# The setup of a one-core kernel's long convolution, cut into eight passes and put between the stages of its first two trips

## The chip, the cores and the metric

One core of a Trainium2 chip runs the whole program. The core has five engines, each with a queue of its own that is worked off in order: TensorE (PE: matmuls, and PEld: its weight loads), VectorE (DVE), ScalarE (ACT), GpSimd (POOL) and SyncE (SP), which here issues nearly all DMAs. They meet at semaphores. The time is the device time in microseconds (us) of one execution: 1694.19 us, the median of 3 runs (1694.01 to 1695.35).

## The reference

Eight sequences of 512 tokens with 256 channels go through two layers, each an attention part and a feed-forward part, with residuals:

```python
x = x + L0_xattn(layernorm(x), ctx, ...)  # 8 heads, 64 context rows, softmax
x = x + L0_ffn(layernorm(x), ...)         # 16 experts of 64, the best 4 by a sigmoid gate
x = x + L1_xattn(layernorm(x), ctx, ...)  # below
x = x + L1_ffn(layernorm(x), ...)         # 8 experts of 1024, each takes the 512 best of 4096 rows
```

The third part attends to the context with the best 32 of 64 scores in each of 4 heads, makes a scale and a shift from it (FiLM), runs a long convolution over the sequence, then FiLM again, a gelu layer and a layernorm. The kernel of the convolution depends on weights alone, not on `x`:

```python
dtA = dt[:, None] * A                      # 256 channels x 64 complex states
dC = C * (jnp.exp(dtA) - 1.0) / A
powers = jnp.exp(dtA[:, :, None] * jnp.arange(L))
K = 2.0 * jnp.einsum('dn,dnl->dl', dC, powers).real
y = irfft(rfft(x, n=2 * L) * rfft(K, n=2 * L))[:, :L] + x * D_skip
```

## The kernel before, in words

The program has three blocks with a barrier between them.

The first, `setup_block` (L113), makes what depends on weights alone. SyncE loads the parameters of the convolution and then all weights (L169 to L189). VectorE computes steps and coefficients on 128x256 tiles (L282 to L318). Then the powers are made in four passes of 64 channels, each as a product of a wide factor (32 steps of 16 tokens, 128x2048) and a narrow one (16 tokens, 128x1024): VectorE makes the phases (`phases`, L329: the products L332 and L334, the rounding L325 and L326), GpSimd the exponents (L232), ScalarE takes sines (L409 to L411) and exponentials (L413, L414), VectorE multiplies them (`powers`, L338), and TensorE sums over the states with 64 small matmuls (L437). Between passes 2 and 3 weights are centred (so that the layernorms' means drop out of the products): TensorE L444 and L456, ScalarE L418 to L426. At the end the taps are transposed twice (L462, L468), transformed (L474) and folded into `kf` (L387 and the adds behind it).

The second, `layers_block`, runs the batches as a pipeline of trips. A batch passes three phases, ATTEND (L0 attention and its gates), MID (L0 feed-forward, L1 attention scores and the best-32 picking) and LAST (FiLM, convolution, gelu layer, scores for the experts), and is in one of them in each trip. One hand-written list, `ORDER`, gives the order in which every engine's queue gets the stages of the three batches; `take_stages` (L496) walks it. The first trip has an ATTEND batch alone, the second an ATTEND and a MID batch, six trips have all three, then come a trip with MID and LAST and one with LAST alone. Stages by name: `soften` (row maximum, subtraction, sum), `attend` (scores, Exp, transposes of the probabilities), `attend_out` and `attend_sum`, `route` and `gates`, `spread` (gates to DRAM and back, spread over partitions as `gT`), `mlp` and `relu`, `pick` (16 in a batch: MAX8 and MATCH_REPLACE, L991 and L995), `picked`, `film`, `transform`, `product`, `back`, `gelu`, `ffn_out`. In PSUM, banks 0 to 3 belong to ATTEND and `mlp`, 4 and 5 to MID, 6 and 7 to LAST.

The first products of a trip's `film` stage are two transposes of `am` (L1408), one for each half; where a trip is said to begin here, it is with one of them. Matmuls of these stages carry one line, L1283, transposes L1289; they are told apart by their tiles (`ps<-m,xT`: attention scores; `ps<-hT,vo`: attention output; `ps<-x,keys` and `ps<-hT,values`: the feed-forward; `ps<-w,big`: `ffn_out`; `ps<-wfilm,v1T`: stage `text` part 2).

The third, `experts_block`, chooses the rows of each expert and runs the eight experts. The change does not touch it.

## Time and profile before

| what | us |
|---|---|
| median of 3 runs | 1694.19 |
| the profiled execution: its own time | 1691.25 |
| its span, first to last instruction | 1689.1 |
| setup block | 0 to 178.0 |
| first trip (ATTEND) | 178.0 to 230.6 |
| second trip (ATTEND, MID), until the second `am` transposes of the third | 230.6 to 343.63 |
| one of the six full trips | 140.2 |
| MID and LAST trip | 110.2 |
| LAST alone | 98.2 |
| experts | 1390.7 to the end |

Busy shares over the span: PE 79%, PEld 48%, DVE 55%, ACT 28%, POOL 19%. A row of a timeline gives start, duration, engine, line, output<-inputs, shapes and count, and in brackets how long the engine had been idle before and what it waited for. Float32 matmuls show two records each. The granted clock of TensorE is 1.00 at 2.4 GHz and 0.50 at 1.2 GHz.

### The profile page before, as it was taken

Reading aid. Unit: us, or ns where it says so; the run is one execution under the profiler, and the core shown is the slowest. Engines: PE = TensorE matmul, PEld = TensorE weight load, DVE = VectorE, ACT = ScalarE, POOL = GpSimd, SP = SyncE. Lnnn points to the kernel's source line nnn. Section 1 sums busy time; section 2 is a strip of 40 time slices with the busy share of each in tenths; the row PEclk is TensorE's granted clock in tenths of the full one; section 3 lists DMA queues with packets and bytes.
Section 4 is the critical chain, followed back from the end, with each engine's and each line's share of the span. In section 5 each row is a group of like instructions: output and inputs, shape, how many; then the busy total and the mean of one; then the engine's idle time right before and its main releaser. Section 6 shows DMA issues by size and latency. Waiting matters only on the chain. (4 is left out here: it accounts for less than half of the span.)

```text
span 1689.1 us, 17636 instructions
## 1 busy us (share of the span) xinstructions
PE 1330.4 (79%) x5358; PEld 810.5 (48%) x5358; DVE 929.4 (55%) x3400; ACT 480.8 (28%) x823; POOL 327.1 (19%) x592
## 2 busy tenths in 40 slices
PE   0265669699889979979988997997995551999997
PEld 0245434345545555455554554545543240667674
DVE  6955414777576567666757656766666428211111
ACT  0433201214322521621532342162142223332221
POOL 3210100203101120320320112022022120433322
PEclk9995779799979969979997996997996675899999
DMA  8000020020020020002003002001200005243511
GB/s 261 2 0 1 2 63 15 14 50 15 14 76 16 12 78 15 1 26 64 16 13 77 16 13 76 14 1 23 54 1 26 1 32 183 67 116 82 144 17 21
DMA packets 44856, 72.55 MB, mean 43 GB/s; under 512 B 8085, under 2 KB 26648, under 8 KB 44634
## 3 DMA queue, kind: packets, MB, share of 16 engines
q1 hardware_dynamic: 38618, 62.90, 12.7%
q0 software_dynamic: 6144, 8.52, 2.9%
q8 instruction: 43, 0.70, 0.2%
q14 instruction: 51, 0.42, 0.1%
HBM read 58.31 MB, written 13.11 MB: 42 GB/s over the span
## 5 line engine op out<-in xcount | busy, mean ns | idle before, releaser
L770 POOL TENSOR_SCALAR ve<-mv 128x2 f32<-128x2 f32 x80 | 18.1, 227 | 854.1 <-DVE mv L868 853.9
L1283 PE MATMUL ps<-x,keys 128*128 128x512 f32 x256 | 137.1, 662 | 11.1 <-DVE hT L954 11.1
L1283 PE MATMUL ps<-zT_second,w 128*128 128x512 f32 x256 | 119.1, 602 | 3.7 <-ACT big L1249 2.4
L1366 PE MATMUL ps<-hT,values 128*128 128x512 f32 x256 | 119.1, 593 | 0.0
L1809 PE MATMUL experts_ps<-experts_yT,experts_fc 128*128 128x512 f32 x256 | 113.5, 602 | 1.3 <-ACT experts_yT L1732 1.3
L1283 PE MATMUL ps<-w,big 128*128 128x256 f32 x512 | 113.6, 381 | 0.8 <-ACT big L1249 0.8
L1821 PE MATMUL experts_ps<-experts_fc,experts_hT 128*128 128x256 f32 x512 | 112.1, 380 | 0.8 <-ACT experts_hT L1744 0.8
L1283 PEld LDWEIGHTS ps<-w,big 128*128 128x128 f32 x512 | 96.6, 190 | 22.7 <-issue 8.5
L1821 PEld LDWEIGHTS experts_ps<-experts_fc,experts_hT 128*128 128x128 f32 x512 | 96.6, 190 | 14.7 <-ACT experts_hT L1744 1.6
L437 PE MATMUL pk<-setup_WA,setup_U 128*32 128x16 f32 x512 | 27.9, 214 | 93.5 <-DVE setup_WA L346 93.5
L1707 DVE SCALAR_TENSOR_TENSOR experts_o<-experts_ps,experts_wh,experts_b2w 128x256 f32<-128x256 f32 x32 | 15.5, 484 | 140.2 <-PE experts_ps L1821 140.2
L1283 PE MATMUL ps<-vf,amT 65*128 65x512 f32 x128 | 80.9, 744 | 14.4 <-ACT amT L1139 13.6
L1283 PEld LDWEIGHTS ps<-x,keys 128*128 128x128 f32 x256 | 51.8, 210 | 78.3 <-issue 57.0
L1744 ACT ACTIVATE experts_hT<-experts_ps,experts_b 128x512 f32<-128x512 f32 x64 | 44.0, 687 | 157.3 <-PE experts_ps L1809 157.3
L954 DVE SCALAR_TENSOR_TENSOR hT<-ps,gT 128x512 f32<-128x512 f32 x64 | 42.6, 687 | 78.8 <-PE ps L1283 62.9
L1587 POOL DMA_INDIRECT out_x<-experts_o,experts_idx x32 | 51.4, 1606 | 157.1 <-DVE experts_o L1707 155.2
L1366 PEld LDWEIGHTS ps<-hT,values 128*128 128x128 f32 x256 | 48.8, 191 | 62.1 <-issue 58.2
L1809 PEld LDWEIGHTS experts_ps<-experts_yT,experts_fc 128*128 128x128 f32 x256 | 48.8, 193 | 60.4 <-issue 60.2
L995 DVE MATCH_REPLACE8 work<-rest,work 128x64 f32<-128x64 f32 x384 | 76.0, 209 | 0.2 <-issue 0.2
L900 DVE SCALAR_TENSOR_TENSOR x<-ps,b_oT,xT 128x512 f32<-128x512 f32 x16 | 12.0, 751 | 111.8 <-PE ps L1283 111.8
L437 PEld LDWEIGHTS pk<-setup_WA,setup_U 128*32 128x32 f32 x512 | 27.6, 157 | 93.7 <-issue 93.7
L1283 PEld LDWEIGHTS ps<-zT_second,w 128*128 128x128 f32 x256 | 46.0, 193 | 48.3 <-issue 42.0
(382 smaller groups left out, 2590.7 us busy)
## 6 DMA issues: line engine op xcount, KB each, us to landing
gT<-expert_gates SPq DMA_DIRECT2D x16, 1024.0 KB, 9.7
experts_fc<-in_fc1T SPq DMA_DIRECT2D x8, 1024.0 KB, 5.4
experts_fc<-in_fc2T SPq DMA_DIRECT2D x8, 1024.0 KB, 9.6
expert_table<-tb SPq DMA_DIRECT2D x8, 528.0 KB, 12.2
x<-in_x SPq DMA_DIRECT2D x8, 512.0 KB, 3.5
xT<-in_xT SPq DMA_DIRECT2D x8, 512.0 KB, 3.6
out_x<-x SPq DMA_DIRECT2D x8, 512.0 KB, 11.5
w<-in_W SPq DMA_DIRECT2D x2, 1024.0 KB, 13.5
```

What stands on the lines that cost most here:

```text
L437: last = nc.tensor.matmul(pk[q * LI:(q + 1) * LI, half, at:at + LJ], Us[q % 2][:, d, :], WAs[q % 2][:, d, :], start=True, stop=True)
L770: nc.gpsimd.tensor_scalar(o, i, c, None, ALU.add).then_inc(*tick(*event))
L900: nc.vector.scalar_tensor_tensor(xp[:, k, :], bank("OT", k), S["b_oT"][:, k:k + 1], xT[:, k, :], ALU.add, ALU.add).then_inc(*tick("emptied ...
L954: nc.vector.scalar_tensor_tensor(hT[:, c % RING, :], bank("H", c), 0.0, gT[:, c, :], ALU.max, ALU.mult).then_inc(*tick("emptied", "H", c))
L995: nc.vector.match_replace(work[:, t, h, :], best[:, h, :], src[:, h, :], OUT_OF_RANGE).then_inc(*tick("tmr", t, n, h))
L1283: last = nc.tensor.matmul(o, l, r_, start=start, stop=stop)
L1366: last = nc.tensor.matmul(bank("O2", k), S["values"][:, c, k * P:(k + 1) * P], hT[:, c % RING, :], start=(c == 0), stop=(c == HC - 1))
L1587: g.indirect_dma_start(out_rows, bass.IndirectOffsetOnAxis(ap=idx[:, e, c:c + 1], axis=0), o[e % 2][:, c, :], None, compute_op=ALU.add).th ...
L1707: nc.vector.scalar_tensor_tensor(o[s][:, c, :], o_bank(CC * e + c), wh[s][:, c:c + 1], b2w[s][:, c, :], ALU.mult, ALU.add).then_inc(out_ma ...
L1744: nc.scalar.activation(hT[e % 2][:, m, :], g_bank(m), ACT.Gelu_apprx_tanh, bias=b1[:, e, m:m + 1]).then_inc(hidden_made, 1)
L1809: last = nc.tensor.matmul(g_bank(m), fc1[e % 3][:, k, m * P:(m + 1) * P], yT[e % 2][:, k, :], start=(k == 0), stop=(k == DC - 1))
L1821: last = nc.tensor.matmul(o_bank(at), hT[e % 2][:, m, c * P:(c + 1) * P], fc2[e % 3][:, m, :], start=(m == 0), stop=(m == HC - 1))
```

## The change

`setup_block` goes. Its buffers are laid over tiles that the first two trips do not use yet (`big`, `xf`, `yv`, `x3`, `tb`, `zT_second`, `work`), and it uses PSUM banks 4 to 7 until the stages of MID and LAST need them. Its work becomes stages of a fourth phase, `KERN`: `steps`, `means`, `masks`, `phases` p and `powers` p (p from 0 to 7, 32 channels each, so tiles of 128x1024 and 128x512), `centre` 0 to 5, `bias`, `fold_film`, `film_row`, and `kernel` 0 to 5 (transposes, transform and folding). Loads get a semaphore for each group in place of one for all, with waits `if first(b)` where the first batch uses them. There are five stage lists now: `FIRST` (ATTEND and KERN up to `powers` 3), `SECOND` (ATTEND, MID and the rest of KERN), `ORDER`, changed in places, for the six full trips, `DRAIN` and `FINAL`. In `FIRST` the stages stand in this order: steps 0, keys 0, steps 1, means, phases 0, centre 0, powers 0, phases 1, masks, keys 1, keys 2, phases 2, centre 1, norm, attend 0, centre 2, soften 0, powers 1, attend 1, attend 2, soften 1, centre 3, soften 2, soften 3, attend 3, bias, attend 4, soften 4, phases 3, attend_out, attend_sum, centre 4, route, powers 2, gates 0, fold_film, gates 1, centre 5, gates 2, phases 4, gates 3, spread, film_row, powers 3. `SECOND` begins text 0, mlp 0, phases 5, text 1, mlp 1, powers 4, relu 0 to 2.

TensorE's queue from the program's start before, all of the setup up to the transform's transposes:

```order
L437 MATMUL pk<-setup_WA,setup_U 32x16 x128
L444 MATMUL pc<-b_ffn,w 128x1 x16
L456 MATMUL pc<-keys,setup_cen 128x512 x8
L456 MATMUL pc<-w,setup_cen 128x512 x8
L456 MATMUL pc<-sel,setup_cen 128x16 x4
L456 MATMUL pc<-gate_w,setup_cen 128x8 x4
L437 MATMUL pk<-setup_WA,setup_U 32x16 x128
L462 MATMUL pt<-ident,setup_kq 64x128 x16
```

And now, in the first trip, from the first batch's first score product; `xf,big` are the 32 matmuls of one pass (powers 1), `keys,work` and `gate_w,work` are centring, `b_ffn,w` is the bias:

```order
L1336 MATMUL ps<-mrow,ones_bf 128x512
L1336 MATMUL ps<-m,xT 128x512 x2
L1381 MATMUL ps<-keys,work 128x512 x4
L1353 MATMUL ps<-xf,big 32x16 x32
L1336 MATMUL ps<-mrow,ones_bf 128x512
L1336 MATMUL ps<-m,xT 128x512 x2
L1342 MATMUL ps<-ident,e_buf 128x128 x4
L1336 MATMUL ps<-mrow,ones_bf 128x512
L1336 MATMUL ps<-m,xT 128x512 x2
L1342 MATMUL ps<-ident,e_buf 128x128 x4
L1381 MATMUL ps<-gate_w,work 128x8 x4
```

The matmuls of the passes, 128 in a row before, now stand by 32 between the score products, with the centring beside them.

VectorE's queue at the start of the second trip now: phases 5, powers 4 (rows L697 to L785 with `xf`, `yv`) and the first six `relu` rows (`hT<-ps,gT`), phases 6 behind them:

```order
L763 SCALAR_TENSOR_TENSOR xf<-tb,yv 128x512
L762 TENSOR_SCALAR tb<-yv,offB 128x512
L763 SCALAR_TENSOR_TENSOR yv<-tb,yv 128x512
L697 TENSOR_TENSOR xf<-xf,zT_second 128x512
L697 TENSOR_TENSOR yv<-yv,zT_second 128x512
L700 TENSOR_TENSOR xf<-xf,yv 128x512
L784 TENSOR_TENSOR big<-big 128x1024
L785 TENSOR_TENSOR xf<-xf,x 128x512
L942 SCALAR_TENSOR_TENSOR hT<-ps,gT 128x512 x6
L771 TENSOR_TENSOR big<-zT_second,it_i 128x1024
L762 TENSOR_SCALAR tb<-big,offA 128x1024
L763 SCALAR_TENSOR_TENSOR big<-tb,big 128x1024
```

Before, the `relu` rows followed the gates' last row with only two small copies between.

In a full trip, TensorE before, at the end of the gelu layer's first product:

```order
L1283 MATMUL ps<-zT_second,w 128x512 x2
L1289 MATMUL ps<-ident,e_buf 128x128 x4
L1283 MATMUL ps<-zT_second,w 128x512 x4
L1283 MATMUL ps<-wfilm,v1T 64x512 x4
L1283 MATMUL ps<-w,big 128x256 x16
L1283 MATMUL ps<-hT,vo 128x512 x8
```

and now:

```order
L1336 MATMUL ps<-zT_second,w 128x512 x2
L1336 MATMUL ps<-wfilm,v1T 64x512 x4
L1342 MATMUL ps<-ident,e_buf 128x128 x4
L1336 MATMUL ps<-zT_second,w 128x512 x4
L1336 MATMUL ps<-w,big 128x256 x16
L1336 MATMUL ps<-hT,vo 128x512 x8
```

The four matmuls of `text` part 2 moved ahead of the last transposes of the probabilities. On VectorE in the same trips `norm_out` 0 now stands ahead of the three last `pick` stages that follow `attend_sum`.

```diff
-def setup_block(nc, ctx, S, A, tally):
...
+ATTEND, MID, LAST, KERN = range(4)
...
+PASSES, PC = 8, 32
...
+FIRST = [
+    (KERN, "steps", 0), (ATTEND, "keys", 0), (KERN, "steps", 1), (KERN, "means"), (KERN, "phases", 0), (KERN, "centre", 0),
...
+SECOND = [
...
+    (MID, "relu", 1), (MID, "relu", 2), (MID, "mlp", 2), (MID, "mlp", 3), (MID, "relu", 3), (MID, "mlp", 4), (MID, "mlp", 5),
...
+            sp.dma_start(ctx0[:], ctx_h[0]).then_inc(*tick("ctx0_loaded"))
+            load("wk", kv_in)
+            load("wv", kv_in)
+            for rows_ in (slice(0, NS), slice(NS, P)):
+                for dst, src in ((are, A["A_reT"]), (aim, A["A_imT"]), (cre, A["C_reT"]), (cim, A["C_imT"])):
+                    sp.dma_start(dst[rows_, :], src).then_inc(par_in, 16)
+            sp.dma_start(ldt, A["log_dt"].partition_broadcast(P)).then_inc(par_in, 16)
...
-            take_stages(stages, 0, None, None)
-            take_stages(stages, 1, 0, None)
+            take_stages(stages, FIRST, 0, None, None, 0)
+            take_stages(stages, SECOND, 1, 0, None, 0)
             for b in range(B - 2):
-                take_stages(stages, b + 2, b + 1, b)
-            take_stages(stages, None, B - 1, B - 2)
-            take_stages(stages, None, None, B - 1)
+                take_stages(stages, ORDER, b + 2, b + 1, b, None)
+            take_stages(stages, DRAIN, None, B - 1, B - 2, None)
...
+            def phases(_, p):
+                if p == 0:
+                    g.wait_ge(*at(0, "k_coef"))
+                else:
+                    g.wait_ge(*at(0, "k_ex", p - 1))
+                if p >= 2:
+                    g.wait_ge(*at(0, "k_pow", p - 2))
+                some = decay[:, p * PC:(p + 1) * PC].unsqueeze(2)
+                g.tensor_tensor(UEs[p % 2], some.to_broadcast([P, PC, LI]), it_i[:].unsqueeze(1).to_broadcast([P, PC, LI]), ALU.mult)
+                g.tensor_tensor(WEs[p % 2], some.to_broadcast([P, PC, LJ]), it_j[:].unsqueeze(1).to_broadcast([P, PC, LJ]),
+                                ALU.mult).then_inc(*tick("k_ex", p))
...
+            def phases(_, p):
+                k = p % 2
+                wide = spare[:, 0:PC * LI].rearrange("p (d i) -> p d i", i=LI)
+                narrow = spare[:, 0:PC * LJ].rearrange("p (d j) -> p d j", j=LJ)
+                if p >= 2:
+                    v.wait_ge(*at(0, "k_taps", p - 2))
+                step(nc.vector.tensor_tensor(Us[k], over(spin, p, LI), it_i[:].unsqueeze(1).to_broadcast([P, PC, LI]), ALU.mult))
+                step(whole_less(Us[k], Us[k], offA[:], wide))
+                step(nc.vector.tensor_tensor(WBs[k], over(spin, p, LJ), it_j[:].unsqueeze(1).to_broadcast([P, PC, LJ]), ALU.mult))
+                step(whole_less(WAs[k], WBs[k], offA[:], narrow))
+                whole_less(WBs[k], WBs[k], offB[:], narrow).then_inc(*tick("k_phase", p))
+
+            def powers(_, p):
+                k = p % 2
+                v.wait_ge(*at(0, "k_sin", p))
+                mul(WAs[k], WAs[k], over(alpha, p, LJ))
+                mul(WBs[k], WBs[k], over(beta, p, LJ))
+                add(WAs[k], WAs[k], WBs[k])
+                v.wait_ge(*at(0, "k_exp", p))
+                nc.vector.tensor_tensor(Us[k], Us[k], UEs[k], ALU.mult)
+                nc.vector.tensor_tensor(WAs[k], WAs[k], WEs[k], ALU.mult).then_inc(*tick("k_pow", p))
+
+            def means(_):
...
+            def bias(_):
+                v.wait_ge(bias_filled, 1)
+                v.wait_ge(w1_in, 80)
+                nc.vector.tensor_tensor(S["b1"][:], S["b1"][:], pc[:, 0, 0:HC], ALU.add).then_inc(bias_made, 1)
...
+            def phases(_, p):
+                k = p % 2
+                if p == 0:
+                    a.wait_ge(*at(0, "k_coef"))
+                a.wait_ge(*at(0, "k_phase", p))
+                nc.scalar.activation(Us[k], Us[k], ACT.Sin, scale=-TWO_PI, bias=sinA[:])
+                nc.scalar.activation(WAs[k], WAs[k], ACT.Sin, scale=-TWO_PI, bias=sinA[:])
+                nc.scalar.activation(WBs[k], WBs[k], ACT.Sin, scale=-TWO_PI, bias=sinB[:]).then_inc(*tick("k_sin", p))
+
+            def powers(_, p):
+                k = p % 2
+                a.wait_ge(*at(0, "k_ex", p))
+                nc.scalar.activation(UEs[k], UEs[k], ACT.Exp)
+                nc.scalar.activation(WEs[k], WEs[k], ACT.Exp).then_inc(*tick("k_exp", p))
+
...
+            def powers(_, p):
+                lanes = slice((p // 2) * LI, (p // 2 + 1) * LI)
+                pe.wait_ge(*at(0, "k_pow", p))
+                for d in range(PC):
+                    last = nc.tensor.matmul(pk[lanes, p % 2, d * LJ:(d + 1) * LJ], Us[p % 2][:, d, :], WAs[p % 2][:, d, :], start=True, stop=True)
+                last.then_inc(*tick("k_taps", p))
+
...
-            setup_block(nc, ctx, S, A, None)
```

## Rows read from the trace of the kernel before

**Rows 1.** Windows by stage: us, busy time (instructions) per engine, granted clock, DMA share, GB/s
```profile
core 0: us, PE busy (x) PEld busy (x) DVE busy (x) ACT busy (x) POOL busy (x), PEclk, DMA share, GB/s
0.00:178.00 178.00, 65.11 (x640) 51.92 (x640) 117.03 (x118) 50.56 (x47) 36.70 (x37) 0.87 0.20 63
178.00:230.60 52.60, 38.06 (x145) 24.86 (x146) 16.75 (x55) 10.24 (x19) 7.30 (x10) 0.76 0.04 12
230.60:343.63 113.03, 84.43 (x272) 43.66 (x272) 56.11 (x283) 18.44 (x38) 12.54 (x26) 0.82 0.18 42
613.29:753.50 140.21, 124.77 (x446) 73.17 (x445) 91.17 (x377) 46.08 (x81) 25.54 (x58) 0.90 0.12 32
```
**Rows 2.** Timeline, a 64-channel pass beside GpSimd and alone: start us, us, engine, line
```profile
32.53 3.63 POOL L232 TENSOR_TENSOR setup_UE<-setup_decay,setup_it_i 128x2048 f32<-128x2048 f32 x1 [25.81 <-DVEq L318]
32.54 5.77 DVE L332 TENSOR_TENSOR setup_U<-setup_turn,setup_it_i 128x2048 f32<-128x2048 f32 x1
38.35 2.83 DVE L325 TENSOR_SCALAR setup_US<-setup_U,setup_offA 128x2048 f32<-128x2048 f32 x1
41.21 5.60 DVE L326 SCALAR_TENSOR_TENSOR setup_U<-setup_US,setup_U 128x2048 f32<-128x2048 f32 x1
50.50 1.22 DVE L326 SCALAR_TENSOR_TENSOR setup_WA<-setup_WS,setup_W 128x1024 f32<-128x1024 f32 x1
53.81 2.29 DVE L332 TENSOR_TENSOR setup_U<-setup_turn,setup_it_i 128x2048 f32<-128x2048 f32 x1
56.14 1.29 DVE L325 TENSOR_SCALAR setup_US<-setup_U,setup_offA 128x2048 f32<-128x2048 f32 x1
```
**Rows 3.** Timeline, VectorE on 512 columns
```profile
171.58 0.69 DVE L257 TENSOR_TENSOR setup_U<-pt,setup_US 128x512 f32<-128x512 f32 x1
```
**Rows 4.** Timeline, ScalarE in the passes
```profile
57.91 1.28 ACT L413 ACT_TABLE_LOAD   x1
59.20 1.91 ACT L413 ACTIVATE setup_UE<-setup_UE 128x2048 f32<-128x2048 f32 x1
67.05 1.13 ACT L410 ACTIVATE setup_WA<-setup_WA,setup_sinA 128x1024 f32<-128x1024 f32 x1
```
**Rows 5.** Timeline, TensorE in the setup
```profile
72.37 6.98 PE L437 MATMUL pk<-setup_WA,setup_U 128*32 128x16 f32 x128 [72.37 <-DVE setup_WA L346]
87.68 6.99 PE L444 MATMUL pc<-b_ffn,w 128*128 128x1 f32 x32
```
**Rows 6.** Timeline of the first two trips
```profile
191.18 1.98 PE L1283 MATMUL ps<-m,xT 128*128 128x512 f32 x4
209.52 8.94 PE L1283 MATMUL ps<-hT,vo 128*128 128x512 f32 x16 [0.68 <-ACT hT L1139]
230.83 0.57 ACT L1139 COPY lists<-ps 16x512 f32<-16x512 f32 x1 [5.10 <-PE ps L1289]
245.80 1.29 DVE L954 SCALAR_TENSOR_TENSOR hT<-ps,gT 128x512 f32<-128x512 f32 x2 [15.88 <-DMA gT<-expert_gates]
343.63 0.38 PE L1408 MATMUL ps<-ident,am 128*64 128x128 f32 x2
```
**Rows 7.** Windows, one of the first trip, three of a steady trip
```profile
208.00:212.00 4.00, 3.32 (x7) 1.61 (x7) 0.00 (x0) 0.59 (x1) 0.00 (x0) 0.50 0.02 4
613.29:633.00 19.71, 17.34 (x47) 9.57 (x46) 9.42 (x30) 3.44 (x8) 0.00 (x0) 0.67 0.63 164
633.00:730.00 97.00, 92.80 (x317) 50.83 (x316) 62.07 (x250) 34.91 (x57) 15.62 (x30) 1.00 0.03 8
730.00:753.50 23.50, 14.64 (x85) 12.77 (x85) 19.68 (x99) 7.72 (x17) 9.91 (x28) 0.69 0.06 21
```
**Rows 8.** Waits of TensorE in one steady trip (613.29 to 753.5)
```profile
PE ps L1289 <- DVE x L1118: 4.8, 1, 4.8
PE ps L1289 <- DVE sct L1126: 3.4, 1, 3.4
```
**Rows 9.** Timeline, the last transposes of the probabilities in that trip
```profile
705.76 0.66 PE L1289 MATMUL ps<-ident,e_buf 128*128 128x128 f32 x4 [0.76 <-POOL e_buf L794]
```

790 lines of the change are left out of this document (425 added, 365 removed).

## The prediction
> **What bounds the kernel now.** I read the busy time by stage first, because a share over the whole span mixes stages with different limits. In the setup VectorE is busy 117.03 of 178.00 us and TensorE 65.11; in the first trip they stand at 16.75 and 38.06 of 52.60, in the second (until the second `am` transposes of the third trip) at 56.11 and 84.43 of 113.03; in a full trip at 91.17 and 124.77 of 140.21 [rows 1]. So the setup is VectorE's, the trips are TensorE's, and up to 343.63 us [rows 6] neither is full: VectorE works 117.03 + 16.75 + 56.11 = 189.9 us there, TensorE 187.6. The two kinds of work have different limits and don't need each other until `kf` is used by the first LAST batch. The experts, from 1390.7 on, keep their work and their time.
>
> Next I read the timeline of the passes, for what one instruction costs beside other engines and alone; then that of the first two trips, for the places where VectorE stands still; then the granted clock in the trips; last the waits of TensorE in a steady trip.
>
> **The change part by part.** The reference point is the second `am` transposes of the third trip, 343.63 us before. I sum up VectorE's time to it, since everything in the new front passes through its queue.
>
> *Start.* VectorE's first product on the parameters can begin at about 12 us. Its loads now stand behind three others, but before it worked through the masks first, so the start is where it was. Term: 12.
>
> *VectorE's work.* 189.9 us move over [rows 1]. In it are slow instructions: in the first pass VectorE ran beside GpSimd's exponents, and the wide product took 5.77 us where the next pass, alone, took 2.29; the subtraction's two rows took 2.83 against 1.29 and 5.60 against 2.29 [rows 2]. That is 3.48 + 1.54 + 3.31 = 8.3 us, which I take out and price anew below: 181.6. Eight passes in place of four double the count at half the size. 128x1024 takes 1.22 us where 128x2048 takes 2.29 [rows 2], so two halves cost 0.15 more than one whole, and 128x512 takes 0.69 [rows 3], so two cost 0.16 more. With some eleven such instructions in an old pass that is 4 x 11 x 0.16 = 7. The 44 more instructions have a gap of their own to the one that they depend on, and the centring's copies and the steps are cut finer: I take 13 for these, an estimate, with 5 and 20 as its ends. Term: 181.6 + 20 = 202.
>
> *Contention with GpSimd.* One old pass lost 8.3 us while GpSimd made the exponents of two old passes, which are four new ones: 2.1 each. GpSimd now makes the exponents of pass p + 1 just as VectorE's phases or powers run, so I count all eight: 16. Below, it could be 4 (only the first two); above, 22. The rows show the wide product longer by 3.48 us beside a GpSimd product of 3.63 [rows 2], so it lost nearly all of the other's duration. The Trainium skill, "SBUF — State Buffer", section "Who interferes with whom", calls the port pair that the two share an exclusive lock; the trace agrees. By that rule each new pass costs VectorE the full duration of GpSimd's two products, an estimate of 2.8 us, 22 in all, and the sum would be 6 us higher.
>
> *VectorE's waits.* These replace the old ones (15.88 us for the gates' DMA before the first `relu` [rows 6], the serial ends of the setup). That DMA wait is hidden in the new order: phases 5 and powers 4, some 12 us of VectorE work, stand in front of `relu` 0. What is late instead, in turn:
> - `powers` p waits for ScalarE's exponentials, which stand behind the sines of pass p + 1. A 128x1024 sine takes 1.13, a table load 1.28, a 128x2048 exponential 1.91 [rows 4], half of it about 1.04. Wide and two narrow sines 2.4, load 1.3, two exponentials 1.6 make 5.3; VectorE covers its three narrow products, 2.1, and in some passes norm or softmax work too. I take 2.5 x 8 = 20 (ends 5 and 35).
> - The first batch's softmax waits for scores that stand behind taps 1 and a centring product: 32 matmuls of a half pass are 3.5, half of 6.98 [rows 5]; the centring's four 512-column products and the scores' own cost about 4 and 1.98 [rows 6]. 9.
> - The bias is 6.99 us of TensorE [rows 5] put between scores 3 and 4; soften 4 waits for most of it. 6.
> - Attention output, 8.94 at the low clock [rows 6], and gates: 3 + 2, the rest lies beside phases 3 and 4.
> - phases 5 waits for taps 3: 3.5 [rows 5].
> - `relu` in the second trip: two key and two value products of 1.98 against 1.29 of VectorE per step [rows 6], 2.7 x 4 = 10, less where a pass stands between them.
> - Second batch: pick 0 2.8, scores behind taps 6 and 7 3.5 each, the first kernel transform 2.9. 12.7.
> Together 66 us, of which the last five items, some 46, are TensorE's own speed.
>
> ScalarE's table switches multiply: Sin and Exp alternate in every pass, with Exp of the softmax between. The row shows the load for 1.28 us and the exponential 0.01 us behind it [rows 4]. The Trainium skill, "ScalarE: Activation LUTs", section "What ACT_TABLE_LOAD costs", gives about 1.28 us for the load and 1.38 more for a drain at each switch; on the load the trace agrees, a drain of that size does not follow it in the row. If it were paid ahead of each load, some seven switches on VectorE's path would make the sum 10 us higher.
>
> *The clock.* In the first two trips TensorE was granted 0.76 and 0.82 on average [rows 1], which means that it ran at half rate for 48% and 36% of the time: 208 to 212 shows 0.50 with TensorE busy 3.32 of 4 us [rows 7]. In the new front TensorE's work is thinner, 188 us spread over some 300. If two fifths of the 46 us above are at the low level where I priced them at the high one, the cost is 18; several prices above already hold slow rows (8.94). I take 10 (ends 0 and 20).
>
> Sum: 12 + 202 + 16 + 66 + 10 = 306 us against 343.63, that is -38.
>
> *Steady trips.* TensorE waits 0.76 us for GpSimd's probabilities ahead of their last transposes [rows 9]; `text`'s four products now stand there and fill it. `norm_out` 0 earlier on VectorE lets GpSimd make the second half's `rstd` about 0.7 us earlier, which the 4.8 us wait for `x` (L1118) gets [rows 8]. So about 1.5 us less in a trip by the instructions. But a trip ends and starts at a granted clock of 0.69 and 0.67 and runs at 1.00 between [rows 7]; where that stretch begins and ends isn't set by these two edits. I take half, -0.8 x 6 = -5 (ends -10 and 0). The last two trips, with lists of their own: an estimate of -1, for waits of VectorE like those of [rows 8] that such a trip no longer has.
>
> **Total.** -38 - 5 - 1 = -44. The profiled execution took 1691.25 us (span 1689.1 and 2.15 around it) and becomes 1647. The median of the runs is 2.94 above that execution, so the prediction is 1650.
>
> **The rivals.**
>
> *Better covered.* The waits are 46 instead of 66, the rest stands (12 + 202 + 16 + 46 + 10 = 286): VectorE has norms, gate work and masks to do while ScalarE makes the exponentials, which my walk along the queues may place wrongly. For it: the old order shows idle TensorE and idle VectorE in the same stretches, and the softmax stages are short. Against: the queues are in order, and most `powers` stand right behind VectorE's short stages. Time 1630.
>
> *VectorE alone.* Waits of 40 and no half-rate term: 12 + 202 + 16 + 40 = 270, time 1650 - 36 = 1614. For it: 202 + 16 = 218 us of work is already four fifths of that. Against: the bias, taps and first attention are TensorE's and serial for the first batch.
>
> *The clock keeps the front low, and the trips give nothing.* TensorE in short pieces between waits is granted half rate for most of the front: the 46 us of its items take about 12 more than I priced, front 318; and the steady trips stay at 140.2. Then -26 - 1 = -27 and the time is 1668. For it: 0.76 in the first trip, where TensorE was busy 72% of the time. A front whose passes run one after another because each reuses the buffers of the pass two before would end here too.
>
> *Slower.* The moved products open a second half-rate stretch in every full trip. From 633 to 730 TensorE is at 1.00 with 92.80 of 97 us busy [rows 7]; were 7.5 us of that work at half rate, a trip would take 7.5 longer. It decides from the point at which the six trips lose what the front gains, 38 + 1 over 6 = 6.5 us a trip. With 7.5 us a trip the sum is -38 - 1 + 45 = +6, time 1700. For it: such stretches exist at each trip's ends. Against: the edit takes idle time out of this stretch, it adds none.
>
> **How the numbers follow.** Forecast 1650: 0.47. Better covered, 1630: 0.20. VectorE alone, 1614: 0.12. Low clock in the front, 1668: 0.17. Slower, 1700: 0.04. From the unknown costs of the likeliest case, ends of the powers' waits (-15, +15), contention (-12, +6), gaps (-8, +7), clock (-10, +10) and trips (-5, +5), which won't all fall on one side, its own range is 1636 to 1662. To hold eight of ten it must take in the second case and most of the fourth, and half of the third: 1618 to 1670. A measurement of this kernel tells about 0.2% (3.4 us) from no change; every case but the last is far beyond it: faster 0.95, within 0.01, slower 0.04.
>
> **What would show it.** The second `am` transposes of the third trip stand at about 306 us; at 270 or 286 a better case holds, at 318 or more the clock's. VectorE waits for ScalarE's exponentials about 2.5 us in a `powers` stage, and its wide products of phases take over 1.22 us (up to 3) in most passes; if they take 1.22, the contention term is wrong. Right ahead of `relu` 0 there is no long wait for the gates' DMA; if there is, the spread's DMA is late and my hiding of it fails. The bias keeps VectorE waiting before soften 4. A full trip takes 139.4, within 1 us; one of 147 is the slower case. The experts block takes 298 us as before; if it moves, the whole account is incomplete.

## The result, and the profile after

The changed kernel takes 1686.93 us (median of 5, 1685.06 to 1687.38) against 1695.35 (5 runs, 1694.01 to 1697.18) of the kernel before on the same chip: 0.9947 of it, interval 0.9932 to 0.9961, or 8.4 us less. I had forecast 1650, in a range of 1618 to 1670. The direction was right; the size was five times too large.

The stages of the profiled execution (span 1685.6), columns as in [rows 1]: the front (everything up to the second `am` transposes of the third trip) in two pieces, one of the usual full trips, the one unusual trip, the MID and LAST trip, the last trip, the experts.

```profile
core 0: us, PE busy (x) PEld busy (x) DVE busy (x) ACT busy (x) POOL busy (x), PEclk, DMA share, GB/s
0.00:178.00 178.00, 107.56 (x595) 69.73 (x596) 107.56 (x180) 59.14 (x83) 43.16 (x53) 0.82 0.26 78
178.00:312.00 134.00, 90.81 (x461) 56.97 (x460) 89.32 (x326) 29.87 (x47) 15.46 (x28) 0.76 0.10 25
601.37:744.94 143.57, 127.67 (x446) 75.02 (x445) 91.17 (x375) 43.94 (x78) 25.85 (x58) 0.88 0.12 31
889.25:1027.70 138.45, 122.72 (x445) 72.15 (x444) 90.94 (x375) 43.59 (x78) 25.70 (x58) 0.92 0.12 33
1171.23:1284.76 113.53, 95.47 (x297) 53.86 (x296) 74.95 (x322) 28.95 (x55) 18.96 (x48) 0.89 0.10 30
1284.76:1383.86 99.10, 58.34 (x178) 36.75 (x178) 35.45 (x91) 19.00 (x35) 12.82 (x33) 0.72 0.03 11
1383.86:1685.60 301.74, 244.37 (x1166) 162.82 (x1166) 81.76 (x282) 77.28 (x149) 86.15 (x91) 0.90 0.34 89
```

The balance against the profiled execution before:

| stretch | before | after | difference | forecast |
|---|---|---|---|---|
| front | 343.6 | 312.0 | -31.6 | -38 |
| six full trips | 838.7 | 859.2 | +20.6 | -5 |
| MID and LAST trip | 110.2 | 113.5 | +3.3 | -1, with the next |
| LAST trip | 98.4 | 99.1 | +0.7 | |
| experts | 298.2 | 301.7 | +3.5 | 0 |
| span | 1689.1 | 1685.6 | -3.5 | -44 |

(Rounded rows; the last two trips end where the experts' first load is issued. The profiled execution before was 4.1 us under the median of its five runs and the one after 0.5 above, so the balance shows 3.9 us of the 8.4.) The front did nearly what I had said. Two thirds of its gain was given back in the trips that I had expected to gain by moves in their own list: 138.2 and then five times 140.0 to 140.2 us before, now 145.9, 143.5, 143.6, 144.3, 138.5, 143.5. Work didn't grow: VectorE is busy 91.17 us in either [rows 1], while TensorE is busy 127.67 instead of 124.77 with the same number of instructions and a mean granted clock of 0.88 instead of 0.90.

The trip of 138.5 must be held against its like. The kernel before has one too, its first full trip, at the same clock of 0.92:

```profile
343.63:481.85 138.22, 122.96 (x445) 71.89 (x445) 91.48 (x376) 46.04 (x80) 25.55 (x58) 0.92 0.08 21
```

So at the same clock the new list is 0.2 us longer than the old one, not shorter. The lengths go with the time that the clock stands at 0.50 in a trip: 22.9 and 23.0 us in the trips of 138.2 and 138.5, 27.4 in those of 140.1, 34.3 in those of 143.5.

Where the clock went shows in windows of four us. First two stretches of the trip that starts at 601.37, then the same two of the trip that starts at 889.25:

```profile
609.37:613.37 4.00, 4.00 (x20) 2.66 (x19) 2.29 (x5) 0.26 (x1) 0.00 (x0) 1.00 0.06 20
613.37:617.37 4.00, 2.79 (x10) 1.87 (x10) 3.90 (x8) 1.67 (x6) 0.00 (x0) 0.78 0.00 0
617.37:621.37 4.00, 4.00 (x9) 1.80 (x8) 4.00 (x11) 0.00 (x0) 0.00 (x0) 0.80 0.00 0
681.37:685.37 4.00, 0.91 (x5) 0.87 (x5) 3.88 (x26) 3.46 (x5) 2.54 (x6) 0.81 0.00 0
685.37:689.37 4.00, 4.00 (x9) 1.44 (x8) 3.86 (x31) 3.82 (x8) 1.04 (x1) 0.76 0.00 0
897.25:901.25 4.00, 2.79 (x17) 1.93 (x16) 4.00 (x8) 1.08 (x5) 0.00 (x0) 1.00 0.09 35
901.25:905.25 4.00, 4.00 (x12) 2.19 (x12) 3.90 (x9) 0.60 (x1) 0.00 (x0) 1.00 0.00 0
965.25:969.25 4.00, 0.92 (x5) 0.49 (x5) 3.50 (x23) 3.09 (x5) 2.83 (x8) 1.00 0.00 0
969.25:973.25 4.00, 4.00 (x11) 1.32 (x10) 3.87 (x32) 3.97 (x8) 1.04 (x1) 1.00 0.00 0
```

In the slower trip the clock falls to 0.50 twice for some 3.4 us inside the trip (two neighbouring windows near 0.8 each), and each time TensorE finishes 1.7 us less than at full rate. In the fast trip there are the same two pauses of TensorE (2.79 and 0.92 us busy of 4) and no fall. In the trips before, [rows 7] had 1.00 throughout 633 to 730.

The pauses, in TensorE's timeline of the same trip: the products of the context, the wait for `v1T`, the wait for the probabilities, and what follows.

```profile
612.82 1.06 PE L1336 MATMUL ps<-ctx_second,wv 96*128 96x64 f32 x8
615.10 1.64 PE L1336 MATMUL ps<-k1bd,wq1T 128*128 128x256 f32 x4 [1.21 <-ACT v1T L1252]
616.52 3.11 PE L1336 MATMUL ps<-x,keys 128*128 128x512 f32 x4
684.51 1.11 PE L1342 MATMUL ps<-ident,e_buf 128*128 128x128 f32 x4 [3.09 <-POOL e_buf L619]
685.41 2.80 PE L1336 MATMUL ps<-zT_second,w 128*128 128x512 f32 x4
688.14 3.65 PE L1336 MATMUL ps<-wfilm,v1T 128*64 128x512 f32 x8
691.72 0.66 PE L1342 MATMUL ps<-ident,e_buf 128*128 128x128 f32 x4
696.59 7.17 PE L1336 MATMUL ps<-w,big 128*128 128x256 f32 x32 [0.78 <-ACT big L1301]
```

The key products behind the first pause take 3.11 us where 1.88 is the rule. The wait of 0.76 of [rows 9] is gone as forecast, but 0.78 us of waiting for ScalarE's last gelu result (`big`) has come behind it, which the four products of `text` 2 had covered in their old place: nothing was won. The wait for the probabilities itself is as long as it was before, where no fall followed it:

```profile
702.63 0.66 PE L1289 MATMUL ps<-ident,e_buf 128*128 128x128 f32 x4 [3.08 <-POOL e_buf L794]
```

And the wait for `v1T` is new. I had not seen it: in the list of the full trips both `mlp` 0 and `mlp` 1 now stand ahead of `text` 0, where one of them used to stand behind it, so the key products that used to cover ScalarE's copy of the context products are spent before it.

### The profile page after: what moved, and what is told of

Same layout as the page of the kernel before. It is cut to its first block and busy times, and to the rows that moved or that the text cites. A ratio compares the mean times of both kernels' runs of the same rounds, so it can differ in the third digit from the quotient of the medians.

```text
span 1685.6 us, 17715 instructions
## 1 busy us (share of the span) xinstructions
PE 1360.9 (81%) x5358; PEld 828.3 (49%) x5358; DVE 935.8 (56%) x3450; ACT 477.0 (28%) x837; POOL 330.9 (20%) x600
## 5 line engine op out<-in xcount | busy, mean ns | idle before, releaser
L1336 PE MATMUL ps<-x,keys 128*128 128x512 f32 x256 | 142.4, 685 | 0.3 <-DVE hT L942 0.3
L1336 PE MATMUL ps<-zT_second,w 128*128 128x512 f32 x256 | 124.9, 627 | 2.7 <-ACT big L1301 1.4
L1941 PE MATMUL experts_ps<-experts_yT,experts_fc 128*128 128x512 f32 x256 | 113.3, 601 | 1.3 <-ACT experts_yT L1864 1.3
L1336 PEld LDWEIGHTS ps<-w,big 128*128 128x128 f32 x512 | 96.6, 190 | 27.4 <-ACT big L1301 9.6
L1839 DVE SCALAR_TENSOR_TENSOR experts_o<-experts_ps,experts_wh,experts_b2w 128x256 f32<-128x256 f32 x32 | 15.5, 484 | 140.2 <-PE experts_ps L1953 140.2
L1336 PE MATMUL ps<-vf,amT 65*128 65x512 f32 x128 | 81.2, 747 | 13.2 <-ACT amT L1183 12.3
L1336 PEld LDWEIGHTS ps<-x,keys 128*128 128x128 f32 x256 | 56.2, 221 | 66.4 <-issue 63.5
L1353 PE MATMUL ps<-xf,big 128*32 128x16 f32 x512 | 27.2, 210 | 58.2 <-DVE xf L785 58.2
L1336 PE MATMUL ps<-m,xT 128*128 128x512 f32 x128 | 71.1, 682 | 0.0
## 6 DMA issues: line engine op xcount, KB each, us to landing
expert_table<-tb SPq DMA_DIRECT2D x8, 528.0 KB, 12.1
out_x<-x SPq DMA_DIRECT2D x8, 512.0 KB, 11.3
```

What stands on the lines that cost most here:

```text
L1336: last = nc.tensor.matmul(o, l, r_, start=start, stop=stop)
L1353: last = nc.tensor.matmul(pk[lanes, p % 2, d * LJ:(d + 1) * LJ], Us[p % 2][:, d, :], WAs[p % 2][:, d, :], start=True, stop=True)
L1839: nc.vector.scalar_tensor_tensor(o[s][:, c, :], o_bank(CC * e + c), wh[s][:, c:c + 1], b2w[s][:, c, :], ALU.mult, ALU.add).then_inc(out_ma ...
L1941: last = nc.tensor.matmul(g_bank(m), fc1[e % 3][:, k, m * P:(m + 1) * P], yT[e % 2][:, k, :], start=(k == 0), stop=(k == DC - 1))
```

## The experiments

Theory A: the new list gives TensorE a pause early in each full trip, and pauses let the granted clock fall; the fall, not the pause, is the cost. Rival B: the new front leaves something behind that slows the trips. Rival C: the half-rate stretches have nothing to do with idle time. (A trip's number below is its length; each experiment's expectation stands first and names its own theories and rivals.)

### The old list in the changed kernel's full trips

```diff
-ORDER = [ (LAST, "film_in", 0), (LAST, "film", 0), (MID, "mlp", 0), ...
+ORDER = [ (LAST, "film", 0), (MID, "mlp", 1), (LAST, "film", 1), ...      # the list of before, word for word
```

> The changed kernel with the six full trips walked by the old stage list; the new front, the two last trips' own lists and everything else stay. Theory A (the new list costs the trips half-rate time): the profile after has 143.5 us in five of six trips and 138.45 in the sixth, and two stretches of about 3.4 us of half rate each that the trips before did not have, one after a TensorE wait of 1.21 us for v1T, one at the wait of 3.09 us for the probabilities. With the old list both go, a trip takes 140.1 us, granted clock 0.90, and the kernel 1687 - 5 x 3.4 + 1 x 1.7 = about 1671 us, within 4. Rival B (the new front itself leaves something behind that slows the trips: tiles in other places, more waits on semaphores of loads): trips stay at 143 and the time at 1685 to 1690.

1668.17 us, 0.9825 of before (0.9808 to 0.9841). Its second full trip, and then its first:

```profile
452.32:592.41 140.09, 124.83 (x445) 73.16 (x444) 91.20 (x375) 46.02 (x80) 25.54 (x58) 0.90 0.12 32
```

```profile
309.95:452.32 142.37, 126.94 (x444) 74.11 (x445) 91.21 (x376) 46.01 (x80) 25.58 (x58) 0.88 0.06 15
```

Its front ends at 309.9, its full trips take 142.4, then 139.7 to 140.7. A holds, and B is refuted for five of the six trips. In the first, B has its share: the new front leaves TensorE at half rate for the trip's first 10 us, where the old front left it at 1.00, and that trip takes 4.2 us more than the 138.2 before. So of the 20.6 us that the full trips lost, some 4 are the front's and some 16 the list's. The kernel with the new front and the old list is about 30 us under the kernel before; over the whole kernel the new list costs 17 to 21 us, by spans or by ratios.

### The new list in the kernel before

```diff
-    for phase, name, *t in ORDER:
+    for phase, name, *t in (FULL if None not in batches else ORDER):      # FULL: the new list
```

> The kernel before with the new list in the six full trips alone; setup, first two trips and the two last ones are as before. Theory A: the trips go from 140.1 to about 143.5 us at a granted clock of 0.88, the kernel from 1695 to 1695 + 6 x 3.4 = about 1715 (1708 to 1716 if one or two trips escape the extra stretches). Rival B (the trips are slower because of the new front): they stay at 140 or 139, the kernel at 1688 to 1696.

1713.22 us, 1.0089 (1.0072 to 1.0106): 15 us slower. Trips of 138.5, 143.5, 143.5, 143.4, 144.4, 138.5: the pattern of the changed kernel, without its front. This is the mirror of the first run: the list alone costs 13.2 us in the six trips, and at the clock of 0.92 its trips are 0.26 us longer than the old list's 138.22. The last two trips have the old list here, and the MID and LAST trip takes 110.3.

### One stage moved back: mlp 1

```diff
-    ... (LAST, "transform"), (MID, "mlp", 1), (LAST, "film_in", 1),
-    (MID, "text", 0), (LAST, "fold"), (MID, "text", 1), ...
+    ... (LAST, "transform"), (LAST, "film_in", 1),
+    (MID, "text", 0), (LAST, "fold"), (MID, "mlp", 1), (MID, "text", 1), ...
```

> The changed kernel with one stage moved in the list of the full trips: mlp 1 behind fold, so that two of the key products stand again between the products of the context and text 1, where TensorE waits 1.21 us for v1T now. Theory A: the wait goes and with it the first half-rate stretch (1.7 us a trip and the 1.2 of idle time less some 1 us that comes back elsewhere): trips of about 141 to 142, the kernel at 1675 to 1680. Rival B: the half-rate stretch there is not caused by that wait; it stays, trips stay at 143.5 minus at most the wait, 1680 to 1687.

1668.45 us, 0.9829 (0.9812 to 0.9845), more than I expected: one stage gives back all that the whole list had cost. Five of the full trips take 139.9 to 140.0. But one pause with a half-rate stretch is left, at the probabilities:

```profile
670.00:674.00 4.00, 0.91 (x5) 0.89 (x5) 3.91 (x26) 3.49 (x5) 2.54 (x6) 0.79 0.00 0
674.00:678.00 4.00, 4.00 (x7) 1.30 (x6) 3.85 (x31) 3.83 (x8) 1.04 (x1) 0.50 0.00 0
678.00:682.00 4.00, 4.00 (x9) 1.01 (x8) 2.24 (x22) 1.13 (x2) 0.00 (x0) 0.86 0.01 2
```

The trip begins at 1.00 instead. Its half-rate time, 6.8 us at the probabilities and 20.5 at the end, is 27.3 us where a trip before had 27.4, and its length is nearly the same too. So the fall at the second pause doesn't need the first: the first is gone here, and the second is followed by a longer fall.

### text 2 moved back

```diff
-    (LAST, "gelu", 5), (MID, "text", 2), (ATTEND, "attend", 4), ...
-    (ATTEND, "soften", 4), (MID, "pick", 1, 3), ...
+    (LAST, "gelu", 5), (ATTEND, "attend", 4), ...
+    (ATTEND, "soften", 4), (MID, "text", 2), (MID, "pick", 1, 3), ...
```

> The changed kernel with text 2 moved back behind pick 1,2 in the list of the full trips, so that the four 64-column products no longer stand ahead of the last transposes of the probabilities. Theory A1 (this move makes the second half-rate stretch, since the wait of 3.09 us and the 0.76 now fall in one place): the second stretch goes, 1.7 us a trip less, kernel about 1677. Theory A2 (the stretch comes from the wait of 3.09 us, which both kernels have, and from where the trip's start lies against the chip's clock decisions): it stays, the wait of 0.76 comes back, and the time is 1684 to 1692.

1681.65 us, 0.9902 (0.9885 to 0.9918), between the two expectations. Trips of 144.9, 145.3, 138.6, 140.2, 142.5, 145.3, only 2.4 us less than in the changed kernel together; 3.6 us are the MID and LAST trip's, which takes 109.9 here. The second stretch stays in four of the six (A2), in two of them for 6.8 us, and is absent in those of 138.6 and 140.2. The move of `text` 2 is not what made it. The trip of 140.2 has both pauses (1.21 and 3.09 us) without a fall.

### The waits left in, TensorE kept at work in them

The changed kernel with its own list, and this helper ahead of two waits of the full trips. It transposes the identity n times, a result that nobody reads, into a place in PSUM that the next product overwrites:

```diff
+            def fill(b, n, *use):
+                pe.wait_ge(*open_(b, *use))
+                for _ in range(n):
+                    nc.tensor.transpose(bank(*use)[:, 0:P], ident[:], ident[:])
...
                 if part == 1:
+                    if 1 <= b <= 6:
+                        fill(b, 8, "MM1")
                     pe.wait_ge(*at(b, "emptied", "KV1"))
...
                     t = s - 1
+                    if s == 3 and b >= 2:
+                        fill(b, 22, "PT", t)
                     pe.wait_ge(*at(b, "pr", t))
```

> The changed kernel, its lists untouched, with TensorE kept at work during two of its waits in the full trips: 8 transposes of the identity ahead of the wait for v1T (1.21 us) and 22 ahead of the wait for the probabilities (3.09 us), written to places in PSUM that the next product overwrites. They take nothing away from the waits. Theory A (idle TensorE makes the clock fall, and the fall is the cost): both extra half-rate stretches go although the waits stay and TensorE has more to do; the trips go from 143.5 to 138.5 to 140, the kernel from 1687 to about 1664. Rival C (the half-rate stretches come from elsewhere, for instance at set times or from all the work done so far, and idle time has no part in it): the clock stays 0.88 and the time 1685 to 1690, more if the added work raises it.

1670.35 us, 0.984 (0.9823 to 0.9856): 18 us less than the changed kernel (0.9947), by adding work. At the two places, and one whole trip:

```profile
606.81:610.81 4.00, 3.67 (x18) 2.42 (x18) 3.90 (x7) 1.68 (x6) 0.00 (x0) 1.00 0.00 0
610.81:614.81 4.00, 4.00 (x11) 1.80 (x10) 4.00 (x11) 0.00 (x0) 0.00 (x0) 1.00 0.00 0
674.81:678.81 4.00, 3.29 (x14) 1.53 (x13) 3.84 (x31) 3.97 (x8) 1.91 (x3) 1.00 0.00 0
678.81:682.81 4.00, 4.00 (x14) 1.49 (x13) 3.88 (x37) 3.63 (x6) 0.18 (x1) 1.00 0.00 0
594.81:734.93 140.12, 127.93 (x476) 76.94 (x475) 90.99 (x375) 43.75 (x78) 25.93 (x58) 0.90 0.12 32
```

`v1T` and the probabilities come no earlier, and the clock stays at 1.00: C is refuted. This is the run that turns "the clock was lower" into a cause. A had 1664, six less: after a first trip of 142.7 the trips take 139.9 to 140.4, the old list's length at the old list's clock (0.90), at the upper end of its 138.5 to 140.

### mlp 1 moved back and the last pause filled

```diff
     # on the kernel with mlp 1 behind fold
+                    if s == 3 and b >= 2:
+                        fill(b, 22, "PT", t)
```

> The kernel with mlp 1 moved back (1668.5 us, trips of 139.9), with 22 transposes ahead of the wait for the probabilities. That kernel still has one half-rate stretch at this wait. Theory A: it goes, 1.7 to 2 us a trip, trips of about 138.2, kernel about 1658. Rival (a trip's length is set by the stretch of half rate at its end, which grows by what is gained before it): trips stay at 139.9, 1668.

1670.8 us, 0.9844 (0.9828 to 0.986): no gain over 0.9829. The rival took it. The half-rate stretch inside is gone, and the trips still take 141.9, 138.0, 139.2, 139.6, 139.5 and 143.4; half-rate time has come back at the trip's start (0.57 from 735 to 739) and its end, 26.9 us in all in the trip of 139.6, against 27.3 with the stretch inside. What was gained inside these trips was given back around their ends, which were at half rate in every trip so far.

### The trips' ends filled

```diff
             def scores(b, h):
+                if h:
+                    fill(b, 28, "xt3", h)
...
+                fill(b, 4, "SC")
                 pe.wait_ge(*at(b, "emptied", "xt3", 1))
...
+                fill(b, 28, "ST")
                 pe.wait_ge(*at(b, "sc1"))
...
+                fill(b, 6 if h == 0 else 3, "FI", 2 * h)
                 pe.wait_ge(*at(b, "emptied", "AT", h))
```

> The same as key_product_back_and_wait_filled and fills at a trip's end too: 28 transposes ahead of the wait for x (4.3 us), 4 ahead of the gates' product, 28 ahead of the wait for sct (3.7 us), 6 and 3 ahead of the FiLM products. Theory A: TensorE is granted 1.00 through the trip's end; gate product 3.6 to 1.9, turns 2.1 to 1.1, FiLM products 3.8 to 1.9, key product 2.9 to 1.9 us are 5.7 less on TensorE, of which some turns into longer waits: 3 to 5 us a trip, trips of 134 to 136, the kernel at about 1635. Rival: what is waited for there is VectorE's chain, which no clock of TensorE shortens; 1 us a trip or less, 1652 to 1658.

This stands on top of the run before it. 1645.05 us, 0.9695 (0.9679 to 0.9711). One trip, and TensorE's timeline at its end (`ident` alone is the fill):

```profile
722.96:858.06 135.10, 128.14 (x536) 80.01 (x537) 90.82 (x376) 43.77 (x78) 25.77 (x58) 0.99 0.13 33
```

```profile
844.13 1.95 PE L1336 MATMUL ps<-gate_w,zT_second 128*128 128x8 f32 x16 [0.24 <-ACT zT_second L1183]
845.94 3.25 PE L1349 MATMUL ps<-ident 128*128 128x128 f32 x28
850.32 0.60 PE L1342 MATMUL ps<-ident,sct 128*8 128x128 f32 x4 [1.12 <-DVE sct L1118]
853.08 1.98 PE L1336 MATMUL ps<-vf,amT 65*128 65x512 f32 x4 [0.85 <-ACT amT L1183]
```

The gates' product takes 1.95 us where the changed kernel has 3.58, and VectorE's chain behind it begins that much earlier. The trips take 135.1 to 137.0 (the first 139.3), three of the six inside A's 134 to 136; the total missed 1635 because I had set out from 1658 and the kernel without these fills stood at 1670.8.

### The same fills in the kernel before

The edit is that of the run above, without the one at the probabilities.

> The kernel before with the fills at the trips' ends alone (wait for x, gates' product, wait for sct, FiLM products). It has no extra half-rate stretch inside its trips. Theory A: the stretch at each trip's end goes (granted clock from 0.90 to 0.98 or more), trips from 140.1 to 136, the kernel from 1695 to about 1671. Rival: without the change's order the ends are bound by VectorE: under 1 us a trip, 1688 to 1695.

1680.39 us, 0.9908 (0.989 to 0.9925): 15 us of the 24 expected. Trips of 139.9, 137.8, 137.5, 135.7, 136.2, 137.4 at 0.93 to 0.99. The half-rate end is a property of the old trips too. Their pause at the probabilities was not filled here, and now the clock falls there in three of the six trips for 3.4 or 6.8 us, some 80 us into the trip, where in the kernel before it stayed at 1.00.

### What GpSimd costs the front

GpSimd makes the exponents for two passes alone, so the convolution's kernel that comes out is not the reference's; the run is only for its time.

```diff
+                n = PC if p < 2 else 1
+                some = some[:, 0:n, :]
...
-                nc.scalar.activation(UEs[k], UEs[k], ACT.Exp)
+                nc.scalar.activation(UEs[k], UEs[k], ACT.Exp, scale=1.0 if p < 2 else 0.0)
```

> The changed kernel with GpSimd's exponents made for passes 0 and 1 alone; for passes 2 to 7 it writes one channel of 32, and ScalarE's exponentials keep their size and give 1. So the kernel of the convolution is not the reference's. It tells what sharing with GpSimd costs VectorE in the front: my sum had 16 us for eight passes; in the trace VectorE's four kinds of instructions of the phases are 11 us over their time alone. Theory A: six passes without it, VectorE 8 us less, of which the powers' waits for ScalarE take some: second am transposes of the third trip at 303 to 308 instead of 312, time 1679 to 1684 (or less, if the trips' starts meet the clock better). Rival: VectorE's slower instructions lie in the shade of its waits, front at 311 to 312, time 1686.

1684.84 us, 0.9926 (0.991 to 0.9943), between A's 1684 and the rival's 1686. The front ends at 306.8 instead of 312.0: 5.2 us, inside what A gave for it (303 to 308), and it decides for A. The trips keep their lengths (145.9, 143.5, 143.6, 144.3, 138.5, 143.5) although they all start 5 us earlier. So the place of the fast trip isn't set by the time since the start.

### The front filled

```diff
+                for _ in range((0, 30, 10, 40, 30, 15, 40, 60)[p]):
+                    nc.tensor.matmul(pk[lanes, p % 2, 0:P], ident[:, 0:LI], ident[:], start=True, stop=True)
                 pe.wait_ge(*at(0, "k_pow", p))
...
+                if b < 2:
+                    fill(b, 40, "GT")
                 pe.wait_ge(*at(b, "gate"))
```

This stands on top of trip_ends_filled, with 20 and 45 transposes ahead of two waits for probabilities in the first two trips.

> trip_ends_filled (1645 us) with fills in the first two trips too: 10 to 60 small products of the identity ahead of the waits of TensorE for the powers of passes 1 to 7, 20 and 45 transposes ahead of two waits for probabilities, 40 ahead of the two waits for the gates. Theory A: in the trace of the changed kernel passes 6 and 7 show VectorE waiting 7.1 us for scores where my sum had 3.5, since 3.6 of taps are followed by scores products of 3.8 us at half rate that take 1.98 at full rate; with the clock at 1.00 such items shrink, second am transposes of the third trip at 300 to 305 instead of 310, time 1636 to 1640. Rival: the matmuls of the taps are bound by their weight loads (3.6 us at either clock) and the fills come too late or too long: 308 to 314, no gain.

1637.7 us, 0.966 (0.9644 to 0.9676). Pass 7 in the changed kernel (taps, mask row, scores), and then with the fills:

```profile
237.80 3.59 PE L1353 MATMUL ps<-xf,big 128*32 128x16 f32 x64 [8.59 <-DVE xf L785]
241.32 0.60 PE L1336 MATMUL ps<-mrow,ones_bf 1*128 1x512 bf16 x1
241.86 3.78 PE L1336 MATMUL ps<-m,xT 128*128 128x512 f32 x4
```

```profile
224.67 13.29 PE L1358 MATMUL ps<-ident 128*32 128x128 f32 x120
237.80 2.17 PE L1361 MATMUL ps<-xf,big 128*32 128x16 f32 x64
239.91 0.39 PE L1336 MATMUL ps<-mrow,ones_bf 1*128 1x512 bf16 x1
240.22 1.98 PE L1336 MATMUL ps<-m,xT 128*128 128x512 f32 x4
```

Taps 2.17 instead of 3.59, scores 1.98 instead of 3.78: 3.2 us less behind VectorE's last product of the pass. But the fill itself, 13.3 us, is longer than the wait was (8.6), and eats the gain: the front ends at 305.2.

### The fills cut to the waits

```diff
-                for _ in range((0, 30, 10, 40, 30, 15, 40, 60)[p]):
+                for _ in range((0, 21, 10, 26, 30, 12, 24, 38)[p]):
```

> front_filled (1637.7 us) with the fills ahead of the powers cut to the waits: 21, 10, 26, 30, 12, 24, 38 in place of 30, 10, 40, 30, 15, 40, 60. In front_filled the taps take 2.17 us in place of 3.60 and the scores product 1.98 in place of 3.78, but 120 records of fills (13.3 us) stand over a wait of 8.6 us in pass 7 and 80 (8.9 us) over one of 5.6 us in pass 6, so that VectorE still waits 7.7 and 6.7 us. Theory A: those fills were the delay; VectorE's waits for the scores of passes 6 and 7 fall to about 4.5 us each, the front ends 6 to 8 us earlier, second am transposes of the third trip at 297 to 300, time 1630 to 1633. Rival: what VectorE gains there it waits for ScalarE's or GpSimd's results next, 303 to 305, time 1636 to 1638.

1633.35 us, 0.9612 (0.9585 to 0.964), runs from 1626.27 to 1637.52. VectorE's waits for the scores of passes 6 and 7 are 3.7 and 5.0 us instead of 6.7 and 7.7, and the front ends at 296.5, a little better than expected; behind the taps of pass 7 the clock falls again, and the scores take 3.28 us. The trips after it vary from 135.1 to 139.8 us. It is the fastest version of this study: 0.9612 where the changed kernel has 0.9947.

### The last trip filled

```diff
+                        if b == B - 1 and h == 0:
+                            fill(b, 125, "YI", h)
...
+                    if b == B - 1 and h == 0:
+                        fill(b, 35, "zt", h)
```

> front_filled with two fills in the last trip: 125 transposes ahead of the wait for the products' rows (17.9 us) and 35 ahead of the wait for z (5.0 us). Theory A: the big,gi products take 2.8 in place of 5.5 us and the turns behind 1.1 in place of 2.2, 3 to 4 us less than front_filled: 1632 to 1637. Rival: the clock is at half rate there for another reason and the fills only delay: equal or up to 3 us more.

1636.53 us, 0.9646 (0.963 to 0.9662), not apart from front_filled. The last trip takes 97.1 us where front_filled has 97.4. The inverse products did become shorter:

```profile
1252.71 13.87 PE L1349 MATMUL ps<-ident 128*128 128x128 f32 x125 [1.55 <-DVE big L1031]
1269.10 3.72 PE L1336 MATMUL ps<-big,gi 128*128 128x256 f32 x16 [2.52 <-DVE big L1072]
```

They take 5.53 us in front_filled. The trip got 0.2 us shorter where 3 to 4 were expected (though the median lies inside the 1632 to 1637 given for A, as it lies inside the rival's range); what took the 1.8 us and the rest I didn't follow up.

## Why the prediction was wrong

**The step that failed** is the term of the steady trips: "by the instructions" 1.5 us less a trip, "I take half, -0.8 x 6 = -5 (ends -10 and 0)". It measured +20.6: some 16 us by the new list (13 in before_new_order), some 4 by the new front's low clock at the first trip's start. Both halves of the term were wrong, the one by the instructions and the one by the clock.

*The instructions.* They gave nothing: 138.45 against 138.22 at the same clock. The 0.76 us went, and 0.78 came in its place; the wait for `x` fell by 0.4 us (4.7 to 4.3) where I had 0.7; and a wait of 1.21 us is new. Of the list's changes I took `text` 2 and `norm_out` 0, and passed over `mlp` 0, which went ahead of `text` 0 and uncovers that wait. With `mlp` 1 moved back in its stead the kernel took 18 us less.

*The price of a pause.* I priced pauses by their length. Here the new one of 1.21 us was followed by 3.4 us at half rate, and so was the one at the probabilities, harmless before at 3.08 us. Filled with work (two_waits_filled), neither was followed by a fall, and the trips were back at 140. So the clock's part, which I had put at half of a small gain, was +3.4 us a trip in the usual ones.

*The argument against the slower rival.* I had written down the mechanism ("the moved products open a second half-rate stretch in every full trip"), with 7.5 us a trip and a chance of 0.04, and dismissed it with "the edit takes idle time out of this stretch, it adds none". It added 1.21 us at `v1T`. The loss was 20.6 us over six trips, half of that rival's price. At 6.5 us a trip it would have taken all the front's gain. The trace of before already showed that the clock's stretches take a fifth of each trip [rows 7]. My "where that stretch begins and ends isn't set by these two edits" held for the stretch at the trips' ends, 23.9 us long before and after; what I left out is that new ones can open inside.

**The last two trips** were forecast at -1 and took +4.0. The MID and LAST trip has the wait for `v1T` and the fall early in it (0.80 and 0.78 in neighbouring windows). Its 3.3 us came with its own new list, `DRAIN`: with the old list in the six trips ahead and the new one here it took 113.3 (trips_old_order), with the new list ahead and the old one here 110.3 (before_new_order).

```profile
1152.56:1265.88 113.32, 95.27 (x297) 53.89 (x296) 74.95 (x322) 28.95 (x55) 18.95 (x48) 0.89 0.10 30
1197.93:1308.26 110.33, 93.24 (x297) 52.92 (x296) 74.72 (x322) 29.07 (x55) 18.95 (x48) 0.90 0.11 31
```

The pause alone didn't do it either: with `mlp` 1 moved back in the six trips, this trip has the same wait of 1.2 us, begins at 1.00 and has no fall, and takes 109.9.

**The front**, point by point. The end, 312.0 against 306, was right within 6 us, by errors that cancel:
- Work and contention on VectorE: 218 forecast, 196.9 busy and some 7 in small gaps, of which 11.3 is contention where I had 16. The rows of the passes' four slowed kinds, mean in ns behind the comma:

```profile
L763 DVE SCALAR_TENSOR_TENSOR big<-tb,big 128x1024 f32<-128x1024 f32 x8 | 13.7, 1714 | 0.3
L771 DVE TENSOR_TENSOR big<-zT_second,it_i 128x1024 f32<-128x1024 f32 x8 | 12.0, 1506 | 4.6 <-PE ps L1353 4.6
L762 DVE TENSOR_SCALAR tb<-big,offA 128x1024 f32<-128x1024 f32 x8 | 9.6, 1196 | 0.3
L773 DVE TENSOR_TENSOR yv<-zT_second,it_j 128x512 f32<-128x512 f32 x8 | 7.0, 875 | 0.3
```

  Alone they take 1.22, 1.22, 0.75 and 0.69 us: 8 x (0.49 + 0.29 + 0.45 + 0.19) = 11.3. Pass by pass VectorE lost 3.0, 2.3, 0, 2.9, 2.4, 0, 0 and 0.6 us. By the rule of the Trainium skill ("SBUF — State Buffer", "Who interferes with whom") I had estimated 22 for eight passes, 2.8 each. Where the two ran side by side the rule's price was about right; what was wrong is that I let all eight do so. GpSimd's products of passes 5 and 6 fell beside waits of VectorE and `relu` rows, which kept their 0.68 us. With six passes' exponents gone the front was 5.2 us shorter.
- VectorE's waits: 66 and 10 for the clock forecast, about 96 measured, and 12.1 ahead of its first instruction, where my 12 for the start stood. (The clock's term rested on "the last five items, some 46"; 46 is the sum of the last six, the last five give 37.) Largest, in the waits of VectorE up to 312:

```profile
DVE mx L873 <- PE ps L1336: 25.5, 6, 7.1
DVE big L784 <- ACT x L1153: 15.3, 5, 4.6
DVE hT L942 <- PE ps L1336: 14.3, 4, 6.0
```

  The scores (`mx`) had 9 + 3.5 + 3.5 and took 25.5: behind each taps product of 3.6 us came a scores product of 3.78, which I had priced at full rate or left out. front_filled shows them at 2.17 and 1.98. The powers' waits for ScalarE, 15.3 and 2.5 for the first pass, were near my 20, the `relu` waits 14.3 against 10.
- The gates' DMA is hidden, as forecast: its row of 15.88 us [rows 6] has no counterpart.
- On the table loads of the Trainium skill ("ScalarE: Activation LUTs", "What ACT_TABLE_LOAD costs"): the powers' waits were not above my sum, and the rows have no room for a drain: in the first pass of the kernel before, the last sine ends at 57.90, the load runs from 57.91 for 1.28 us, and the exponential starts at 59.20. The measurement decides.

**The experts** were forecast unchanged and show 3.5 us more. This is not the change's: the run with the new list in the kernel before has 303.9 and the filled kernel before 301.7, both with the old front, against 298.2 in the one profile before, an execution 2.9 us under its median. What differs is a few waits of 0.6 to 2.2 us at 1426 to 1436, beside GpSimd's indirect loads; their cause stays open.

**Open:** what decides, with the same pauses, that the clock falls in one trip and not in the next. The trip after one of 144.3 or 144.4 was the fast one in three kernels. Nor do the runs show why the pause at the probabilities, of the same length in both lists, was followed by a fall with the new one and by none in the kernel before; with the old list and the trips' ends filled it was too, in three trips of six. They show that at these two places a pause is a necessary part (filled, no fall followed) and not a sufficient one.

## What to carry to other kernels

Price a pause of TensorE by what its clock does behind it: read the granted clock in short windows around each wait before and after, since a list with 1.2 us more of waiting cost 3.4 us a trip here, and no row of the waits shows it. Compare a trip with one at the same clock before calling its instructions faster. When a list of stages changes, go through every swapped pair on the waiting engine; the harmful one was the least conspicuous. And where TensorE must wait, products that nobody reads, written into the place that it will overwrite anyway and cut to the length of the wait, can give more than the reordering does: from 1668.45 us with `mlp` 1 moved back to 1633.35 with the fills, 35 us, where the change itself gave 8.4.

## What the hardware showed that I had not expected

The same two pauses (1.21 and 3.09 us) were followed by a fall of the clock in one trip and by none in another (0.78 and 0.81 against 1.00 and 1.00 above). The trips' lengths went with the time at half rate, in whichever part of the trip it lay: 23 us in those of 138.2 and 138.5, 27.3 to 27.6 in those of 139.9 to 140.2, 34.3 in those of 143.5. Filling a pause inside moved a half-rate stretch to the trip's start and end with hardly a gain (139.9 to 139.5) until the trip's end was kept at work as well (135.1). And the small products of the taps, 64 records of 3.59 us at the low level, take 2.17 at the high one, 0.60 of the time and not half of it.
